# Eight gather buffers, earlier expert weights and rows loaded once in a graph network with experts

## The chip, the cores and the metric

The kernel runs on one core of one Trainium2 chip as a single launch. The metric is the device time of the whole execution, in microseconds. Each time is a median of runs on the same chip; the lowest and the highest stand beside it. The profile is one execution taken by the hardware profiler.

## The reference

A vector of 256 features for each of 3125 nodes passes eight residual parts: four graph layers and four expert layers. Two of the parts matter here. Both contain an attention over the neighbours of each node.

```python
# part L1_ffn: a graph attention chooses the experts (4 heads, 4 experts)
h = (x_flat @ W_gat).reshape(M, HEADS, NUM_EXPERTS)          # 16 numbers for a node
e = leaky_relu(a_src[src] + a_dst[dst], 0.2)                 # one score for edge and head
ee = exp(e - segment_max(e, dst)[dst])
alpha = ee / (segment_sum(ee, dst)[dst] + 1e-16)
agg = segment_sum(h[src] * alpha[:, :, None], dst) + b_gat   # self loops included
for ei in range(4):                                          # all experts for all nodes
    out += g[ei] * (gelu(x @ W1[ei] + b1[ei]) @ W2[ei] + b2[ei])

# part L3_gnn: graph attention, 8 heads of 32; then L3_ffn: 8 experts, top 2
alpha = segment_softmax(leaky_relu(a_src[src] + a_dst[dst], 0.2))
x = x + relu(segment_sum(h[src] * alpha[:, :, None], dst) + bias)
x = x + sum(combine[:, e] * (gelu(norm(x) @ w1[e] + b1[e]) @ w2[e] + b2[e]) for e in range(8))
```

The attention of L1_ffn has 65,536 edges and one loop for each node. That of L3_gnn has 100,000 edges.

## The kernel before

The nodes stand in 25 tiles of 128, one node on each partition. The program is a row of stages. A stage opens its own buffers and semaphores, writes one instruction list per engine, and closes with a barrier of all engines. What one stage does late, no other stage can hide. Within a stage the engines are tied together by counting semaphores alone; the helper `when` waits for a value that is worked out from loop registers.

An early stage sorts the edges by target on the chip and writes a table for each of the two attentions: blocks of `SLOTS` = 8 neighbours for each of the 128 nodes of a tile. `base_row` holds the first block of each tile, and at index NT the total. A tile of the router attention has two or three blocks, one of the head attention four to six. Unused slots of the table hold an index out of bounds, and the gather skips them. Since the loops round up, the table needs empty blocks behind the last one; a DMA from `empty` writes eight of them (one for each table, both waited for on `padded`).

**Stage l1p** (`prepare`) normalises x for the experts and leaves it transposed in `c.xt`. **Stage l1f** (`prepare`) makes the 16 features and the two scores of each node. It writes them to `rows`, sorted for gathering, and to `own_rows`, in the order of the tiles, with 24 numbers a row.

**Stage l1a** (`attend_beside_experts`) does the router's attention beside its experts:

- SP loads block indices for a ring of `BUFFERS` = 4 buffers, then the expert weights (`w1` and `w2`, 2 MB each, and four small bias loads and `b2`). After that it loops over blocks: it waits until a block's eight gathers have landed, signals `arrived`, and loads the indices of the block four later.
- POOL (GpSimd) loops over blocks, rounded up to the ring's length: it waits for `idx_in` and for `freed` (VectorE is done with the buffer), and issues eight indirect DMAs, each of 128 rows of 96 bytes (L2652).
- VectorE runs tiles. In `tile` it waits for the tile's own row and makes the softmax's start state by five operations (L2790 to L2796), which are the self loop. For each block, `edges` computes scores (from L2804), a running maximum and the differences `d`, signals `shifted`, waits for the exponentials on `weighed`, multiplies (L2819, after which the buffer is `freed`) and sums. Behind the first block of each tile but the first stands `empty`, which adds `b2` to the experts' output of the turn before.
- ScalarE runs the same tiles. `attend_tile` waits for `self_free`, issues the dynamic DMA of the own row into one of two slots of `self_rows` (L2709), and computes one exponential a block. Between them stand the experts' four Gelu steps of the turn and, in `store`, the store of y of the turn before. It ends with a wait for the own row. Exponential and Gelu take turns, so ScalarE reloads its function table.
- TensorE runs 20 turns (4 experts, 5 groups of 5 tiles), tied to `hidden` and `used`. So tiles 0 to 19 run beside a turn, and tiles 20 to 24 run without.
- At the end SP writes `found` to `by_gate` in 3200 pieces, and POOL gathers it back by `place` in 25 indirect DMAs.

**Stage l3a** (`attend_heads_beside_experts`) has the same skeleton with rows of 264 numbers. SP loads the four indices (L2218), then all weights of the last eight experts. VectorE fills the four buffers with `FLOOR` (L2397), waits for `loaded`, and handles the tiles. `valued` counts two products a block (L2428), and the second frees the buffer. The experts' work for a group of finished tiles runs beside the next group's attention; L2540 adds an expert's output to x. The last group is a single tile. POOL issues the stores of the finished tiles to `out_dram` (L2261), all behind the gathers in its own order, since they stand behind its loop.

Both loops of POOL and SP have `(total + BUFFERS) // BUFFERS` turns of `BUFFERS` blocks.

## Time and profile before

| | us |
|---|---|
| median of 3 runs | 5790.37 (5789.03 to 5790.59) |
| profiled execution, its own time | 5781.05 |
| span of the profiled execution | 5779.6 |
| TensorE, VectorE, ScalarE, GpSimd busy | 2908.9, 3171.6, 1642.9, 2183.8 |

The costliest groups of instructions on POOL and around the two stages, from the page (line, engine, operation, output<-input, count, then busy us and the mean of one in ns, then idle before and who ended most of it):

```profile
L2253 POOL DMA_INDIRECT l3a_got<-rows,l3a_idx x928 | 976.6, 1052 | 528.4 <-issue 286.9
...
L2652 POOL DMA_INDIRECT l1a_got<-rows,l1a_idx x512 | 510.4, 997 | 318.5 <-issue 159.5
...
L2686 PE MATMUL ps<-l1a_w,l1a_h 128*128 128x256 f32 x800 | 232.3, 432 | 224.1 <-issue 168.3
```

At the start of l3a, the first memset of a gather buffer and the issue of the four index loads on SP's queue (start, duration, engine, then in brackets the idle time before it and who ended it):

```profile
4158.77 1.82 DVE L2397 MEMSET l3a_got<- 128x2112 f32 x1 [0.41 <-issue]
4158.81 1.75 SPq L2218 DMA_DIRECT2D l3a_idx<-table_main  x4
```

Read the groups with the count in mind: 512 gathers are 64 blocks of eight, and the "issue" time of 159.5 us over 512 is the 0.3 us between two gathers. "issue" is time for which the profile shows no wait: the engine's own sequencer took it. A name with a q behind it (SPq, ACTq, DVEq) is an engine's sequencer, which waits, counts and issues DMAs; that time is not in the engine's busy time.

The stages of interest by time: l1p from 2085 to 2128.5, l1f to 2219.5, l1a to 3058 (the placing gathers behind it last until 3090), l3p from 4097 to 4158, l3a from 4158 to 5780.

### The profile page before, as it was taken

Reading aid. Unit: us, or ns where it says so; the run is one execution under the profiler, and the core shown is the slowest. Engines: PE = TensorE matmul, PEld = TensorE weight load, DVE = VectorE, ACT = ScalarE, POOL = GpSimd, SP = SyncE. Lnnn points to the kernel's source line nnn. Section 1 sums busy time; section 2 is a strip of 40 time slices with the busy share of each in tenths; the row PEclk is TensorE's granted clock in tenths of the full one; section 3 lists DMA queues with packets and bytes.
Section 4 is the critical chain, followed back from the end, with each engine's and each line's share of the span. In section 5 each row is a group of like instructions: output and inputs, shape, how many; then the busy total and the mean of one; then the engine's idle time right before and its main releaser. Section 6 shows DMA issues by size and latency. Waiting matters only on the chain. (4 is left out here: it accounts for less than half of the span.)

```text
span 5779.6 us, 67813 instructions
## 1 busy us (share of the span) xinstructions
PE 2908.9 (50%) x15435; PEld 2113.2 (37%) x15474; DVE 3171.6 (55%) x7705; ACT 1642.9 (28%) x2993; POOL 2183.8 (38%) x2146
## 2 busy tenths in 40 slices
PE   0430065895995952566730489958301132343446
PEld 0320064784884841344520234446200111122224
DVE  8876386674776561222224554442455656676663
ACT  0322042773771211223310254322101222222221
POOL 1036212001001526566562100015366656666662
PEclk9999999997996975777865799979655566666678
DMA  0311154543433211111113634432323322332210
GB/s 29 68 32 31 8 195 159 170 131 117 133 95 106 66 57 41 21 25 25 30 23 99 233 128 159 167 98 65 127 71 82 80 68 70 82 79 78 65 43 23
DMA packets 332190, 488.33 MB, mean 84 GB/s; under 512 B 159589, under 2 KB 250259, under 8 KB 330134
## 3 DMA queue, kind: packets, MB, share of 16 engines
q1 hardware_dynamic: 192198, 269.65, 14.9%
q0 software_dynamic: 92304, 177.29, 11.8%
q10 hardware_dynamic: 47552, 39.98, 2.1%
q14 instruction: 100, 0.82, 0.0%
q8 instruction: 36, 0.59, 0.0%
HBM read 375.91 MB, written 137.24 MB: 89 GB/s over the span
## 5 line engine op out<-in xcount | busy, mean ns | idle before, releaser
L2253 POOL DMA_INDIRECT l3a_got<-rows,l3a_idx x928 | 976.6, 1052 | 528.4 <-issue 286.9
L2348 PE MATMUL ps<-l3a_xt,l3a_w 128*128 128x512 f32 (+1 forms) x448 | 268.8, 761 | 739.8 <-ACT l3a_h L2292 492.0
L2652 POOL DMA_INDIRECT l1a_got<-rows,l1a_idx x512 | 510.4, 997 | 318.5 <-issue 159.5
L1581 PE MATMUL ps<-l0a_all_rows,l0a_w 128*128 128x257 f32 x2500 | 556.5, 382 | 28.2 <-DVE l0a_w L1699 28.2
L1581 PEld LDWEIGHTS ps<-l0a_all_rows,l0a_w 128*128 128x128 f32 x2500 | 475.8, 191 | 101.7 <-issue 31.9
L1972 PE MATMUL ps<-l2a_table,l2a_count 128*128 128x512 bf16 x1837 | 411.3, 384 | 61.1 <-DVEq L2067 59.1
L2348 PEld LDWEIGHTS ps<-l3a_xt,l3a_w 128*128 128x128 f32 x448 | 112.0, 276 | 875.6 <-issue 875.4
L2277 ACT ACT_TABLE_LOAD x99 | 127.0, 1283 | 904.5 <-DVEq L2419 583.4
L2686 PE MATMUL ps<-l1a_w,l1a_h 128*128 128x256 f32 x800 | 232.3, 432 | 224.1 <-issue 168.3
L1972 PEld LDWEIGHTS ps<-l2a_table,l2a_count 128*128 128x128 bf16 x1875 | 185.2, 99 | 287.5 <-issue 72.1
L1508 ACT ACTIVATE l0a_low<-ps,l0a_factors x650 | 254.1, 509 | 86.7 <-PE ps L1571 79.1
L2675 PE MATMUL ps<-xt,l1a_w 128*128 x640 | 220.0, 501 | 99.5 <-DMA l1a_b<-in_L_ffn_b_dram 54.8
L2686 PEld LDWEIGHTS ps<-l1a_w,l1a_h 128*128 128x128 f32 x800 | 168.4, 214 | 273.7 <-issue 251.5
L2358 PE MATMUL ps<-l3a_w,l3a_h 128*128 128x256 f32 x800 | 202.9, 410 | 124.1 <-DVEq L2543 93.0
L2428 DVE TENSOR_TENSOR l3a_v<-l3a_got,ps 128x1024 f32 x224 | 263.0, 1215 | 3.6 <-issue 2.9
L2358 PEld LDWEIGHTS ps<-l3a_w,l3a_h 128*128 128x128 f32 x800 | 163.2, 207 | 173.5 <-issue 151.1
L2675 PEld LDWEIGHTS ps<-xt,l1a_w 128*128 128x128 f32 x640 | 140.7, 223 | 187.1 <-issue 145.8
L1090 POOL DMA_INDIRECT rows<-own_rows,node x50 | 48.8, 975 | 416.1 <-DVEq L958 404.2
L2436 DVE TENSOR_TENSOR l3a_v<-l3a_v x112 | 141.1, 1259 | 116.1 <-issue 101.0
L1699 DVE TENSOR_TENSOR l0a_w<-l0a_w,l0a_held 128x1280 f32<-128x1280 f32 x130 | 192.9, 1485 | 13.4 <-DVE xt L1734 13.4
L1882 POOL DMA_DIRECT2D l2a_seen<-l2a_state x13 | 9.1, 704 | 468.3 <-DMA l2a_state<-l2a_seen 398.5
L2713 ACT ACT_TABLE_LOAD x53 | 68.0, 1283 | 351.6 <-issue 239.2
(965 smaller groups left out, 6576.1 us busy)
## 6 DMA issues: line engine op xcount, KB each, us to landing
l0a_held<-counts SPq DMA_DIRECT2D x130, 640.0 KB
counts<-count_held SPq DMA_DIRECT2D x13, 3200.0 KB, 9.7
l2a_held<-counts SPq DMA_DIRECT2D x65, 640.0 KB
l3a_got<-rows,l3a_idx POOLq DMA_INDIRECT x928
l_y<-l1a_y_sb ACTq DMA_DIRECT2D x20, 640.0 KB
l2a_table<-rows SPq DMA_DIRECT2D x16, 640.0 KB
l2a_state<-l2a_seen SPq DMA_DIRECT2D x1, 9984.0 KB
l2a_seen<-l2a_state POOLq DMA_DIRECT2D x12, 768.0 KB, 6.0
```

The source lines that it names most:

```text
L1508: ins = act.activation(low_at(n * Q + q, h), spread_of(n, W, 2 * W), ACT.Copy, scale=factors[:, C, at:at + 1])
L1581: ins = pe.matmul(sums_of(n, k, D + 1), w[:, at, k * P:(k + 1) * P], all_rows[:, at, 1:RW], start=(at == 0), stop=False)
L1699: dve.tensor_tensor(chunk(q), chunk(q), held_of(n, q), ALU.mult).then_inc(weighed, 1)
L1972: ins = pe.matmul(ps[:, bass.ds(parity(b, g) * G + k, 1), :].rearrange("p o n -> p (o n)"), count[:, at, k * P:(k + 1) * P], table[:, part ...
L2253: pool.indirect_dma_start(out=got[:, at:at + RW], out_offset=None, in_=rows[:, :], in_offset=bass.IndirectOffsetOnAxis(ap=idx[:, a, k:k + ...
L2348: ins = pe.matmul(ps[:, m, 0:size * P], w1[:, x, k, m * P:(m + 1) * P], xt[:, 0:size, k, :], start=(k == 0), stop=(k == KT - 1))
L2358: ins = pe.matmul(ps[:, 2 + j // 2, (j % 2) * D:(j % 2 + 1) * D], h[:, x % 2, m, j * P:(j + 1) * P], w2[:, x, m, :], start=(m == 0), stop= ...
L2428: dve.tensor_tensor(valued_of(b)[:, lo:hi, :, 0:DH], buffer(b)[:, lo:hi, 0:D].rearrange("p s (h d) -> p s h d", h=H), p[:, lo:hi, :].unsqu ...
L2436: ch(dve.tensor_tensor(rows[:, 0:4, :, :], rows[:, 0:4, :, :], rows[:, 4:8, :, :], ALU.add))
L2652: pool.indirect_dma_start(out=got[:, at:at + RW], out_offset=None, in_=rows[:, :], in_offset=bass.IndirectOffsetOnAxis(ap=idx[:, a, k:k + ...
L2675: ins = pe.matmul(ps[:, 2 * (m % 2) + q, 0:(hi - lo) * P], w1[:, x, k, m * P:(m + 1) * P], xt[:, bass.ds(i * C + lo, hi - lo), k, :], star ...
L2686: ins = pe.matmul(ps[:, 4 + j // 2, (j % 2) * D:(j % 2 + 1) * D], h[:, m, j * P:(j + 1) * P], w2[:, x, m, :], start=(m == 0 and j % 2 == 0 ...
```

## The change

1. **Rings of eight.** `BUFFERS` = 4 becomes `RING` = 8 in both attention stages: index slots, gather buffers, their semaphores, the first index loads, and in l3a the memsets. The loops of POOL and SP now round up to `(total + 7) // 8` turns of eight blocks. The tables get two empty pads each instead of one, and room for them (`blocks_of`).
2. **Weights ahead.** A new class `Ahead` holds the buffers of the router's expert weights. Their seven DMAs are issued on SP in stage l1p, behind its own loads, and stage l1a no longer has them. The buffers live across the three stages.
3. **Own rows once.** All 25 tiles' own rows come in one DMA into `self_all`, issued by SP in front of the index loads. VectorE makes `ref_all` (leaky relu of the self score) and `init_all` (ones, and the own features) for all tiles in four operations. A tile's prologue is now two copies. ScalarE loses the wait for `self_free`, the dynamic DMA and the wait for `self_in`; `self_free` and `self_in` no longer exist.
4. **One more wait.** `store` on ScalarE now waits on `y_out` until the store before last has landed.

```diff
-BUFFERS = 4
+RING = 8
+class Ahead:
+    def __init__(self, nc, stack, name, w_in, b_in, w_out, b_out):
...
+        self.landed, self.count = nc.alloc_semaphore(f"{name}_landed"), 3 + E
+    def load(self, sp):
+        w_in, b_in, w_out, b_out = self.sources
+        sp.dma_start(self.w1[:, :, :, :], w_in.rearrange("e (k p) n -> p e k n", p=P)).then_inc(self.landed, 16)
+        sp.dma_start(self.w2[:, :, :, :], w_out.rearrange("e (k p) n -> p e k n", p=P)).then_inc(self.landed, 16)
+        for x in range(self.E):
+            sp.dma_start(self.b1[:, x, :], b_in[x, :].rearrange("(k p) -> p k", p=P)).then_inc(self.landed, 16)
+        sp.dma_start(self.b2[:, :, :], b_out.rearrange("(o e) n -> o e n", o=1).broadcast_to([P, self.E, D])).then_inc(self.landed, 16)
...
# the tables
-                    sp.dma_start(s.table[bass.ds(total * (P * SLOTS), P * WIDE), 0].rearrange("(p s) -> p s", s=WIDE), empty[:, :]).then_inc(s.padded, 16)
+                    for k in range(2):
+                        sp.dma_start(s.table[bass.ds((total + k * SLOTS) * (P * SLOTS), P * WIDE), 0].rearrange("(p s) -> p s", s=WIDE),
+                                     empty[:, :]).then_inc(s.padded, 16)
-                    sp.wait_ge(s.padded, 16)
+                    sp.wait_ge(s.padded, 32)
...
# prepare, SP, behind its loads
+                    if ahead is not None:
+                        ahead.load(sp)
...
# both attention stages
-                with pool.Fori(0, (total + BUFFERS) // BUFFERS) as q:
-                    for a in range(BUFFERS):
+                with pool.Fori(0, (total + (RING - 1)) // RING) as q:
+                    for a in range(RING):
...
# l3a, POOL and VectorE
-                        when(pool, c, valued, q * (2 * BUFFERS) + (2 * a + 2))
+                        when(pool, c, valued, q * (2 * RING) + (2 * a + 2))
-                for a in range(BUFFERS):
+                for a in range(RING):
                     ch(dve.memset(buffer(a), FLOOR))
...
# l1a, SP
+                sp.dma_start(self_all[:, :, :], own_rows.rearrange("(t p) w -> p t w", p=P)).then_inc(loaded, 16)
-                    sp.dma_start(w1[:, :, :, :], w_in.rearrange("e (k p) n -> p e k n", p=P)).then_inc(weights_in, 16)
-                    sp.dma_start(w2[:, :, :, :], w_out.rearrange("e (k p) n -> p e k n", p=P)).then_inc(weights_in, 16)
-                    for x in range(E):
-                        sp.dma_start(b1_sb[:, x, :], b_in[x, :].rearrange("(k p) -> p k", p=P)).then_inc(weights_in, 16)
-                    sp.dma_start(b2[:, :, :], b_out.rearrange("(o e) n -> o e n", o=1).broadcast_to([P, E, D])).then_inc(b2_in, 16)
...
# l1a, ScalarE (the added wait is in store)
-                    when(act, c, self_free, t + 1)
-                    act.dma_start(self_rows[:, bass.ds((t % 2) * RW, RW)], own_rows[bass.ds(t * P, P), 0:RW]).then_inc(self_in, 16)
-                    when(act, c, self_in, (t + 1) * 16)
+                    when(act, c, y_out, turn * 16 + 32)
...
# l1a, VectorE, before the tiles
+                dve.wait_ge(weights_in, 16 * ahead.count)
+                ch.add(dve.tensor_tensor(ref_all[:, :, :], own_el, own_er, ALU.add))
+                ch.add(dve.memset(init_all[:, :, 0:H], 1.0))
+                ch.add(dve.tensor_copy(init_all[:, :, H:H + VW], own_h))
+                ch(dve.scalar_tensor_tensor(ref_all[:, :, :], ref_all[:, :, :], SLOPE, ref_all[:, :, :], ALU.mult, ALU.max))
...
# l1a, VectorE, each tile
-                    when(dve, c, self_in, (t + 1) * 16)
-                    ch.add(dve.tensor_copy(er_of[:, :], own(t, VW + H, RW)))
-                    ch(dve.tensor_tensor(top[:, :], own(t, VW, VW + H), own(t, VW + H, RW), ALU.add))
-                    ch.add(dve.scalar_tensor_tensor(e[:, SLOTS, :], top[:, :], SLOPE, top[:, :], ALU.mult, ALU.max))
-                    ch.add(dve.memset(den, 1.0))
-                    ch.add(dve.tensor_copy(acc, own(t, 0, VW)))
+                    ch.add(dve.tensor_copy(e[:, SLOTS:SLOTS + 1, :], ref_all[:, at_t, :]))
+                    ch.add(dve.tensor_copy(both[:, :].unsqueeze(1), init_all[:, at_t, :]))
                     ch.join()
-                    dve.sem_inc(self_free, 1)
...
-        return -(-edges // SLOTS) + 3 * NT + 4 * BUFFERS + 3 * SLOTS
+        return -(-edges // SLOTS) + 3 * NT + 2 * RING + 5 * SLOTS
...
-        prepare(nc, c, "l1p", c.x, None, D, ready=wmat, add=True)
+            ahead = Ahead(nc, held, "l1w", a["L1_ffn_W1"], a["L1_ffn_b1"], a["L1_ffn_W2"], a["L1_ffn_b2"])
+            prepare(nc, c, "l1p", c.x, None, D, ready=wmat, add=True, ahead=ahead)
```

## Rows read from the trace of the kernel before

**Rows 1.** Busy time by window: stage l1p, stage l1a, stage l3a's attention.

```profile
core 0: us, PE busy (x) PEld busy (x) DVE busy (x) ACT busy (x) POOL busy (x), PEclk, DMA share, GB/s
2085.00:2128.50 43.50, 31.93 (x150) 27.26 (x150) 31.70 (x111) 8.86 (x22) 0.00 (x0) 0.80 0.00 1
2219.50:3058.00 838.50, 446.58 (x1440) 309.06 (x1440) 205.84 (x1043) 209.08 (x318) 510.38 (x512) 0.73 0.16 28
4158.00:5660.00 1502.00, 421.83 (x1200) 254.52 (x1201) 943.11 (x2049) 310.27 (x498) 977.48 (x929) 0.62 0.28 74
```

**Rows 2.** Waits, l1a then l3a: who waits <- for whom: us, count, mean.

```profile
POOL l1a_got L2652 <- DVEq L2819: 158.6, 21, 13.7
...
DVE l1a_er_of L2791 <- DMA l1a_self_rows<-own: 142.0, 11, 19.6
...
DVE l1a_er_of L2791 <- issue: 90.1, 11, 14.0
...
POOL l3a_got L2253 <- DVE l3a_v L2428: 233.8, 30, 17.8
```

**Rows 3.** Timeline, POOL, first gather of two bursts: start, duration, [idle before <- releaser].

```profile
2480.37 0.99 POOL L2652 DMA_INDIRECT l1a_got<-rows,l1a_idx  x1 [6.37 <-DVEq L2819]
...
2517.70 0.99 POOL L2652 DMA_INDIRECT l1a_got<-rows,l1a_idx  x1 [6.42 <-DVEq L2819]
```

**Rows 4.** Timeline, PE, DVE and ACT between those bursts, 2500 to 2516.

```profile
2502.70 0.59 PE L2686 MATMUL ps<-l1a_w,l1a_h 128*128 128x256 f32 x1 [2.53 <-issue]
...
2504.06 0.17 DVE L2791 COPY l1a_er_of<-l1a_self_rows 128x4 f32 x1 [9.96 <-issue]
...
2504.80 0.70 ACTq L2709 DMA_DIRECT2D l1a_self_rows<-own  x1
...
2512.56 0.19 DVE L2804 TENSOR_TENSOR l1a_e<-l1a_got,l1a_er_of 128x32 f32<-128x32 f32 x1 [7.82 <-issue]
...
2514.65 5.54 PE L2675 MATMUL ps<-xt,l1a_w 128*128 x12 [0.62 <-issue]
2514.72 1.28 ACT L2713 ACT_TABLE_LOAD   x1 [20.25 <-issue]
```

**Rows 5.** Timeline, start of l1a.

```profile
2224.24 12.87 SPq L2627 DMA_DIRECT2D l1a_b<-in_L_ffn_b_dram  x4
...
2240.94 7.05 PE L2675 MATMUL ps<-xt,l1a_w 128*128 x16 [54.76 <-DMA l1a_b<-in_L_ffn_b_dram]
```

**Rows 6.** Timeline, start of l3a: VectorE's first operation of blocks 0, 3, 4 and 5.

```profile
4183.63 0.23 DVE L2413 TENSOR_TENSOR l3a_e<-l3a_got,er 128x64 f32<-128x64 f32 x1 [13.56 <-issue]
...
4227.40 0.23 DVE L2413 TENSOR_TENSOR l3a_e<-l3a_got,er 128x64 f32<-128x64 f32 x1 [8.58 <-issue]
...
4242.41 0.22 DVE L2413 TENSOR_TENSOR l3a_e<-l3a_got,er 128x64 f32<-128x64 f32 x1
...
4250.29 0.22 DVE L2413 TENSOR_TENSOR l3a_e<-l3a_got,er 128x64 f32<-128x64 f32 x1
```

**Rows 7.** Timeline, VectorE at the end of l1a, tiles 21 to 24.

```profile
2970.44 0.17 DVE L2791 COPY l1a_er_of<-l1a_self_rows 128x4 f32 x1 [1.16 <-DVE l1a_found L2837]
...
3017.29 0.17 DVE L2791 COPY l1a_er_of<-l1a_self_rows 128x4 f32 x1 [0.86 <-issue]
...
3028.05 0.18 DVE L2837 TENSOR_TENSOR l1a_found<-l1a_both,l1a_bias 128x16 f32 x1 [0.77 <-issue]
...
3046.11 0.19 DVE L2804 TENSOR_TENSOR l1a_e<-l1a_got,l1a_er_of 128x32 f32<-128x32 f32 x1 [10.88 <-remote]
...
3053.58 0.17 DVE L2837 TENSOR_TENSOR l1a_found<-l1a_both,l1a_bias 128x16 f32 x1 [0.16 <-DVE l1a_both L2836]
```

**Rows 8.** Timeline, VectorE at the end of l3a.

```profile
5529.36 2.35 DVE L2428 TENSOR_TENSOR l3a_v<-l3a_got,ps 128x1024 f32 x2
...
5621.91 1.66 DVE L2540 SCALAR_TENSOR_TENSOR x<-ps,l3a_g_now,x 128x256 f32 x4 [5.42 <-remote]
...
5684.74 1.66 DVE L2540 SCALAR_TENSOR_TENSOR x<-ps,l3a_g_now,x 128x256 f32<-128x256 f32 x4 [25.11 <-remote]

```

More of the change, by code:

```diff
@@ L2158, in attend_heads_beside_experts @@
         chain_sem, loaded, weights_in, arrived = (sem(n) for n in ("chain", "loaded", "weights_in", "arrived"))
[L2159 to L2160 removed]
+        idx_in = [sem(f"idx_in_{a}") for a in range(RING)]
+        gathered = [sem(f"got_{a}") for a in range(RING)]
         shifted, exped, weighed, valued = (sem(n) for n in ("shifted", "exped", "weighed", "valued"))
@@ L2395, in _ @@
                 dve.memset(warmed[:, :], 0.0).then_inc(warm, 1)
-                for a in range(BUFFERS):
+                for a in range(RING):
                     ch(dve.memset(buffer(a), FLOOR))
@@ L2559, in _, with attend_beside_experts @@
                 ch.restart()
-def attend_beside_experts(nc, c, name, table, base_row, rows, own_rows, bias, tiny, place, agg, w_in, b_in, w_out, b_out, y):
+def attend_beside_experts(nc, c, name, table, base_row, rows, own_rows, bias, tiny, place, agg, ahead, y):
     H, DH = 4, 4
@@ L2619, in load @@
                         "(p s) -> p s", s=SLOTS)).then_inc(idx_in[a], 16)
[L2621 removed]
+                for a in range(RING):
                     load(a, a)
[L2623 to L2630 removed]
+                with sp.Fori(0, (total + (RING - 1)) // RING) as q:
+                    for a in range(RING):
                         when(sp, c, gathered[a], (q + 1) * (16 * SLOTS))
                         sp.sem_inc(arrived, 1)
[L2634 to L2637 removed]
+                        load(q * RING + (RING + a), a)
+                for a in range(RING):
+                    when(sp, c, idx_in[a], ((total + (RING - 1)) // RING + 1) * 16)
                 sp.wait_ge(closed, 1)
@@ L2642, in _ @@
             def _(pool):
-                total = pool.value_load(base_row[0:1, c.NT:c.NT + 1], min_val=1, max_val=blocks - 2 * BUFFERS)
+                total = pool.value_load(base_row[0:1, c.NT:c.NT + 1], min_val=1, max_val=blocks - 2 * RING)
                 last_node = pool.to_reg(c.N - 1)
-                with pool.Fori(0, (total + BUFFERS) // BUFFERS) as q:
-                    for a in range(BUFFERS):
+                with pool.Fori(0, (total + (RING - 1)) // RING) as q:
+                    for a in range(RING):
                         when(pool, c, idx_in[a], (q + 1) * 16)
-                        when(pool, c, freed, q * BUFFERS + (a + 1))
+                        when(pool, c, freed, q * RING + (a + 1))
                         for k in range(SLOTS):
```

92 lines of the change are left out of this document (44 added, 48 removed).

## The prediction

> **What bounds the kernel now.** I read the stage windows first, then who waits for whom in the two attention stages, then single tile changes in the timeline. The kernel is a row of stages with a barrier between them, so a gain counts only in its own stage. The change works in two: l1a (the router attention, 838.5 us) and l3a (head attention, some 1500 us and a tail). In both no engine is busy two thirds of the time: GpSimd (POOL) 510 of 838 us and 977 of 1502 us, TensorE and VectorE less [rows 1]. POOL issues the gathers, 510.38 us for 512 in l1a, 1.0 us each [rows 1], and 0.3 us of issue between them, so 8 of them, one block, take 10.4 us.
>
> A deeper ring pays where the consumer waits for a gather. It does not. In l1a POOL is the one that waits, 158.6 us in 21 waits, for VectorE to free a buffer; VectorE's own waits are for its own rows (142.0 us, 11 times, and 90.1 us of issue) [rows 2]. In l3a POOL waits 233.8 us for a buffer [rows 2]. The ring is full, not empty.
>
> What costs time is odd. POOL starts a burst at 2480.37 and gathers three blocks without a pause, some 31 us; the next starts at 2517.70, after 6.42 us of waiting [rows 3]. So a tile of three blocks takes 37.3 us, burst and pause. Late in a burst all other engines crawl: VectorE idles 9.96 us before its row copy at 2504.06 and 7.82 us more before its first edge operation at 2512.56, and ScalarE's table load comes after 20.25 us of "issue"; meanwhile TensorE stands before single matmuls of 0.59 us, 2.53 us before the one at 2502.70. At 2514.65, some 3.4 us after the burst's end (2517.70 less 6.42), TensorE runs 12 matmuls in 5.54 us [rows 4]. I call this the crawl; the traces show it after 10 to 25 us of unbroken gathers and not its cause.
>
> **The change, part by part.**
> *Weights earlier.* TensorE begins at 2240.94, held by the bias loads, whose issue alone takes 12.87 us on SP [rows 5]; VectorE waits for the same loads, until some 2242. Now SP enters its loop at once, and block 0, whose gathers start as SP issues the biases (2224.24) and last 10.4 us, can be used about 2236.5, some 5.6 us sooner. But the next blocks follow at 10.4 us, so block 1 is not ready before some 2247, about when VectorE comes to it now. Gain 1 us (bounds 0 and 6). The move puts 4 MB and some 14 us of issue on SP's queue in l1p, where SP has nothing else and the DMA share is 0.00 over 43.5 us [rows 1]; its last load needs to land only by 2236, some 110 us later. Cost 0; the 12.87 us of bias issue and what goes with it if that cover were gone. The one load of all own rows replaces 25 small ones; it is first on SP's queue, 12 us or more before block 0 is there: 0. The longer memset (0.7 us more) hides there too.
>
> *Tile change in l1a.* Gone per tile: ScalarE's wait, dynamic DMA and second wait, VectorE's wait and three of its five operations. These operations take 0.2 us or less each (the row copy 0.17 [rows 4]); what they cost is turns in the crawl (ScalarE's DMA holds its queue 0.70 us [rows 4], which I take for each instruction of ScalarE and VectorE) and the row's DMA, queued behind the y store. Since the period is burst plus pause, only the pause can shrink. Of 6.4 us, 3.4 us are the crawl's end, which stays; then ScalarE's table load, its exponential and VectorE's three operations until the buffer is free, the other 3.0 us [rows 3, 4]. With the row's DMA gone ScalarE has 5 of about 11 turns less before that exponential, so it often falls before the crawl ends. I take 2.5 us for each of the 20 tiles beside experts: -50. Bounds: 0 (TensorE's 20 starved instructions come last instead) and 158.6 (no pause at all). The new wait for the store before last stands in front of ScalarE's store and, behind it, the next tile's exponentials; that store was issued a tile (27 us or more) earlier, so 0.
>
> *Rings of eight.* In the steady state buffer b+8 is asked for when b is freed, as b+4 was: 0. What differs is the start and the end. At the start POOL runs four more blocks, 41.7 us, without a pause, and the others crawl longer. In l3a's first burst VectorE starts block 0 at 4183.63, block 3 at 4227.40 and block 4 at 4242.41, and block 5, after it, at 4250.29 [rows 6]: 14.6 us a block in the crawl against 7.9. In 41.7 us that is 2.9 blocks for 5.3, a loss of 19 to 20 us in each stage (bounds 0 and 42): +20 and +20.
> At the end of l1a the last eight blocks, tiles 21 to 24, took 83.1 us from 2970.44 to 3053.58, with gathers nearly to the end: tile 24's first edge operation stood 10.88 us, to 3046.11, until they were over. Uncrawled, a tile takes some 10.7 us (3017.29 to 3028.05, one tile's first operation to its last) [rows 7], four 43. With eight buffers the last three blocks are still gathered once tile 20 frees its buffers, 31 us past it, so I leave 10 us of crawl: -31 (bounds -41 and -10).
>
> *l3a besides.* Four more index loads (the four of now hold SP's queue 1.75 us, in the table's fence) stand before the weights' issue, after which SP first signals a block (VectorE's first block is at 4183.63): +2. Four more memsets (1.82 us each, the same fence) stand in front of that same wait, in which VectorE idles 13.56 us [rows 6]: 0 (bound +8). VectorE handles 112 blocks, POOL gathers 928 / 8 = 116; rounded up to eights it is 112, so 32 gathers vanish. Gathers run into the last tile's own time, and the stores of `out_dram` follow them without a pause. Behind them VectorE stands 25.11 us until 5684.74 [rows 8]; about 4 us of it is TensorE's work. Now the last gathers are block 111's, which start when block 103's product (5529.36 [rows 8]) is done, so POOL is free by 5545 and stores 13 or 17 tiles then: -21 at the tail, -10 for VectorE's gaps in the last tile, 5.42 us at 5621.91 [rows 8] and one like it, +8 for the same stores crawling earlier (bounds 0 and 21).
> The second pad of each table: +1.
>
> Sum: l1a -1 -50 +20 -31 = -62; l3a +2 +20 -21 -10 +8 = -1; pads +1; -62 us. The profiled execution took 5781.05 us, span 5779.6, 9.3 us under the median; it comes to 5719, the median to **5728 us**.
>
> The Trainium skill speaks against the crawl: "SBUF — State Buffer", section "Who interferes with whom", says DMA never contends with a compute engine, and that only GpSimd's descriptor generation is starved, by VectorE. The trace disagrees: gathers stay at 0.99 us while the others slow down [rows 3, 4]. By the page the two first bursts would cost nothing, and the sum would be 40 us lower, 5688; as far as the trace bears it out, 5 of the forecast's 59 in 100.
>
> **Rivals.** *Pauses vanish* (18%): the removed row load was the whole pause. For it: 142.0 and 90.1 us of waits [rows 2]; against: crawl and starved TensorE. l1a is then POOL's 64 blocks of 10.4 us from 2224, 666 us, and 40 us for what the ring still holds: it ends at 2930, not 3054. 124 us less, 5666.
> *Slower: bursts merge* (13%): once ScalarE's exponential comes before a burst's end, POOL starts the next three blocks at once, and the crawl lasts through them. It decides when the others progress at under half speed in 62 us bursts: then a merged pair of tiles takes as long as two now. Transitions 0, first bursts +42 each, end -31, l3a tail -21 -10 +8, start +2, pads +1, -1: +32, 5822.
> *No change* (10%): the tile change is off the path, since TensorE's starved matmuls end last, and the rings' two ends cancel: -62 + 50 = -12, less if the tail's stall only moves (+13): 5791.
> Forecast 59%, own range 5685 to 5770.
>
> **Numbers.** 0.2% is 11.6 us, about what a measurement can tell from no change. The range reaches down near the vanished pauses and up over no change, with 8 and 9 of 100 left outside: 5655 to 5805. Faster: 0.59 x 0.97 and all of the vanished pauses, 0.75. Slower: the merged bursts and a little of no change, 0.14. Same 0.11.
>
> **What would show it.** Right: POOL's pauses in l1a of 3 to 5 us instead of 6.4, and no wait of VectorE for own rows; tiles 21 to 24 in about 52 us; block starts in l3a's first 150 us later than before by 20 us; 896 gathers in l3a, and the step from the last `l3a_stats` to the next sum under 10 us. Wrong: pauses unchanged (the path is TensorE), bursts of six blocks with a period over 75 us (merging), or first bursts no slower (the crawl does not grow with the burst).

## The result, and the profile after

| | before, us | after, us |
|---|---|---|
| median | 5790.34 (5789.03 to 5790.59, 4 runs) | 5906.74 (5899.09 to 5912.77, 4 runs) |
| span of the profiled execution | 5779.6 | 5910.9 |

Ratio 1.0204, 95% interval 1.0188 to 1.0220: 116 us slower, where 62 us faster was forecast and the range ended at 5805.

The two traces laid over each other, stage by stage, give the 131.3 us between the spans: 2.3 us up to l1a's start, 66.9 in l1a, 2.8 between its end and l3a's start, and 59.3 from there. Times since each stage's first memset, from VectorE's operations in the timelines:

| us since the stage's start | before | after |
|---|---|---|
| l1a: first burst of gathers | 9 blocks, 93.5 us | 14 blocks, 145.8 us |
| l1a: tile 1 ends | 120.3 | 174.3 |
| l1a: tile 20 ends | 749.1 | 852.7 |
| l1a: tile 24 ends | 833.6 | 900.5 |
| l3a: first burst of gathers | 7 blocks, 74.1 us | 14 blocks, 149.2 us |
| l3a: tile 1 starts | 114.9 | 171.5 |
| l3a: last block starts | 1477.9 | 1559.1 |
| l3a: end of the kernel | 1621.3 | 1680.6 |

So l1a lost 54 us in the first burst and 50 in its steady state and got 37 back at the end. l3a lost 57 in the first burst and 25 on the way and got 22 back. (The first tiles are larger than was said: tile 0 has five blocks in l1a and seven in l3a.)

Busy time by window in the changed kernel, l1a and l3a's attention (core 0: us, then busy time and count of each engine, TensorE's granted clock, DMA share, GB/s), to lay beside [rows 1]:

```profile
2221.50:3123.00 901.50, 437.47 (x1440) 307.23 (x1440) 199.50 (x972) 207.74 (x318) 512.20 (x512) 0.70 0.12 21
4230.00:5795.00 1565.00, 427.05 (x1158) 257.45 (x1159) 934.80 (x2024) 308.92 (x495) 954.60 (x913) 0.61 0.27 72
```

Nobody works more: POOL's 512 gathers are busy for 512.2 us as before, VectorE's work in l1a is 6 us less, the clock a little lower. What grew is idle time, and the waits say whose (who waits <- for whom: us, times, longest), beside [rows 2]:

```profile
DVE l1a_y_sb L2800 <- DMA l0e_got<-done: 360.7, 20, 34.6
...
POOL l1a_got L2670 <- DVEq L2834: 201.5, 20, 15.8
...
POOL l3a_got L2278 <- DVE l3a_v L2453: 259.7, 31, 20.4
```

VectorE's wait for own rows is gone, as the change says. In its place stands one before `empty` (L2800), 360.7 us in 20 waits. The name behind the arrow is a wrong guess of the profile: by the code these are the waits for `used`, the signal of TensorE's last output matmul of the turn, and for an earlier store of y. In the case below all stores of y issued so far had landed by 2564.2. Timeline of the changed kernel, TensorE, ScalarE and VectorE from 2557 to 2597 (start, us, engine, line, idle before <- releaser):

```profile
2557.53 8.80 PE L2704 MATMUL ps<-l1w_w,l1a_h 128*128 128x256 f32 x40
...
2585.98 0.58 PE L2693 MATMUL ps<-xt,l1w_w 128*128 x1 [2.22 <-issue]
...
2589.81 1.28 ACT L2744 ACT_TABLE_LOAD   x1 [19.51 <-DMA l0e_got<-done]
2590.12 1.62 DVE L2800 TENSOR_TENSOR l1a_y_sb<-ps,l1w_b 128x512 f32 x3 [16.76 <-DMA l0e_got<-done]
...
2592.47 0.19 DVE L2819 TENSOR_TENSOR l1a_e<-l1a_got,l1a_self_all 128x32 f32 x1 [0.73 <-DVE l1a_y_sb L2800]
...
2593.61 1.28 ACT L2728 ACT_TABLE_LOAD   x1 [0.72 <-DVEq L2824]
...
2595.36 0.29 DVE L2828 TENSOR_TENSOR l1a_v<-l1a_got,l1a_p 128x128 f32<-128x128 f32 x1 [1.59 <-ACT l1a_p L2728]
```

And POOL's two burst starts around it:

```profile
2555.34 1.00 POOL L2670 DMA_INDIRECT l1a_got<-rows,l1a_idx  x1 [10.26 <-DVEq L2834]
...
2596.59 0.99 POOL L2670 DMA_INDIRECT l1a_got<-rows,l1a_idx  x1 [10.27 <-DVEq L2834]
```

The last output matmul starts at 2565.95, and VectorE passes its wait for it at 2589.65, just before ScalarE passes one for a product whose matmul started at 2568.1. Until then VectorE has no operation for 16.76 us and ScalarE none for 19.51, until 3.5 us after the burst's last gather (2596.59 less 10.27 is 2586.3).

Are the two engines frozen, or do they wait for a signal? The trace also holds the times at which semaphores were updated. The update of `used` that VectorE waited for is recorded at 2589.62, 23.7 us after the start of its matmul, and the two of `product` at 2589.72 and 2589.81. So by the record they wait for TensorE's signals, and these come late. In all of l1a 36 of the 40 updates of `used` are recorded. Half of them come 12 us or more after the start of the matmul before them, and 29 more than 5 us after it. In the kernel before it is 22 of 40 that come more than 5 us after it. Whether the signal is late, or the matmul itself, whose end is modelled, the trace does not tell. Nor is this all of the crawl: VectorE's gap before 2512.56 in [rows 4] ends without any update from TensorE (the next is recorded at 2514.87).

The period of the tiles is 41.25 us against 37.3 in [rows 3]; the burst is still 31 us, and the pause went from 6.4 to 10.3 us. Of those 10.3, the crawl's end is 3.5 as before. Behind it stand now three adds of `empty` (1.62 us), and then a whole block: scores, table load, exponential, product. Before, the same place held only the second half of a block whose scores were already done (2512.56 in [rows 4]); `empty` came behind POOL's restart, under the burst. The other engines do not work less between two bursts. They are at another point of the tile when the crawl catches them.

The first burst of l3a, VectorE's first operation of blocks 0, 3, 4, 5, 6 and 7 and POOL's first burst, beside [rows 6]:

```profile
4259.74 0.23 DVE L2438 TENSOR_TENSOR l3a_e<-l3a_got,er 128x64 f32<-128x64 f32 x1 [7.96 <-issue]
...
4304.27 0.23 DVE L2438 TENSOR_TENSOR l3a_e<-l3a_got,er 128x64 f32<-128x64 f32 x1 [7.91 <-issue]
4329.67 0.23 DVE L2438 TENSOR_TENSOR l3a_e<-l3a_got,er 128x64 f32<-128x64 f32 x1 [9.30 <-issue]
4354.25 0.23 DVE L2438 TENSOR_TENSOR l3a_e<-l3a_got,er 128x64 f32<-128x64 f32 x1 [7.88 <-issue]
4380.24 0.23 DVE L2438 TENSOR_TENSOR l3a_e<-l3a_got,er 128x64 f32<-128x64 f32 x1 [8.58 <-issue]
4402.57 0.23 DVE L2438 TENSOR_TENSOR l3a_e<-l3a_got,er 128x64 f32<-128x64 f32 x1 [0.50 <-DVE l3a_acc L2469]
```

```profile
4233.44 1.04 POOL L2278 DMA_INDIRECT l3a_got<-rows,l3a_idx  x1 [7.65 <-DVEq L2423]
...
4395.50 1.73 POOL L2278 DMA_INDIRECT l3a_got<-rows,l3a_idx  x1 [12.87 <-DVE l3a_v L2453]
```

POOL gathers from 4233 to 4382.6 without a pause. Deep in the burst VectorE takes 25 us a block, not 14.6, while POOL takes 10.6. One such block was in the trace of before too. From block 2 to block 3 it took 24.5 us (4202.91 to 4227.40), where blocks 0 to 2 together had taken 19.3:

```profile
4202.91 0.23 DVE L2413 TENSOR_TENSOR l3a_e<-l3a_got,er 128x64 f32<-128x64 f32 x1 [6.21 <-issue]
```

Each block that VectorE frees gives POOL another one, so eight buffers became a burst of 14 blocks.

At the end of l3a the step that was expected behind [rows 8] is there. The last tile's sums, with 1.94 us before the one that waited 25.11:

```profile
5806.83 1.66 DVE L2565 SCALAR_TENSOR_TENSOR x<-ps,l3a_g_now,x 128x256 f32<-128x256 f32 x4 [0.41 <-DVE x L2485]
...
5812.69 1.66 DVE L2565 SCALAR_TENSOR_TENSOR x<-ps,l3a_g_now,x 128x256 f32<-128x256 f32 x4 [1.94 <-PE ps L2383]
```

### The profile page after: what moved, and what is told of

It reads as the page before. It is cut to its first block and busy times, and to the rows that moved or that the text cites. A ratio compares the mean times of both kernels' runs of the same rounds, so it can differ in the third digit from the quotient of the medians.

```text
span 5910.9 us, 67346 instructions
## 1 busy us (share of the span) xinstructions
PE 2914.1 (49%) x15435; PEld 2119.0 (36%) x15474; DVE 3170.5 (54%) x7638; ACT 1642.8 (28%) x2993; POOL 2145.7 (36%) x2114
## 5 line engine op out<-in xcount | busy, mean ns | idle before, releaser
L2278 POOL DMA_INDIRECT l3a_got<-rows,l3a_idx x896 | 937.9, 1047 | 540.1 <-issue 272.7
L2670 POOL DMA_INDIRECT l1a_got<-rows,l1a_idx x512 | 512.2, 1000 | 367.0 <-DVEq L2834 201.5
L2693 PE MATMUL ps<-xt,l1w_w 128*128 x640 | 264.6, 553 | 392.2 <-ACT l1a_h L2744 205.0
L2693 PEld LDWEIGHTS ps<-xt,l1w_w 128*128 128x128 f32 x640 | 153.3, 244 | 499.8 <-issue 467.7
L2383 PE MATMUL ps<-l3a_w,l3a_h 128*128 128x256 f32 x800 | 211.3, 422 | 112.5 <-issue 48.1
L2800 DVE TENSOR_TENSOR l1a_y_sb<-ps,l1w_b 128x512 f32 (+1 forms) x60 | 32.4, 596 | 360.7 <-DMA l0e_got<-done 360.7
L2704 PE MATMUL ps<-l1w_w,l1a_h 128*128 128x256 f32 x800 | 179.3, 383 | 36.0 <-issue 35.6
L2704 PEld LDWEIGHTS ps<-l1w_w,l1a_h 128*128 128x128 f32 x800 | 153.9, 193 | 58.3 <-issue 36.9
```

Of the source, the lines that this page charges most:

```text
L2278: pool.indirect_dma_start(out=got[:, at:at + RW], out_offset=None, in_=rows[:, :], in_offset=bass.IndirectOffsetOnAxis(ap=idx[:, a, k:k + ...
L2383: ins = pe.matmul(ps[:, 2 + j // 2, (j % 2) * D:(j % 2 + 1) * D], h[:, x % 2, m, j * P:(j + 1) * P], w2[:, x, m, :], start=(m == 0), stop= ...
L2670: pool.indirect_dma_start(out=got[:, at:at + RW], out_offset=None, in_=rows[:, :], in_offset=bass.IndirectOffsetOnAxis(ap=idx[:, a, k:k + ...
L2693: ins = pe.matmul(ps[:, 2 * (m % 2) + q, 0:(hi - lo) * P], w1[:, x, k, m * P:(m + 1) * P], xt[:, bass.ds(i * C + lo, hi - lo), k, :], star ...
L2704: ins = pe.matmul(ps[:, 4 + j // 2, (j % 2) * D:(j % 2 + 1) * D], h[:, m, j * P:(j + 1) * P], w2[:, x, m, :], start=(m == 0 and j % 2 == 0 ...
```

## The experiments

The chips differ. Each set of runs was compared with the kernel before on its own chip. I call the chip of the result A. The others were B to G, six different ones; A may be one of them.

| chip | kernel before, median | l1a, last tile ends | tile of three blocks |
|---|---|---|---|
| A (result) | 5790 | 834 | 37.4 |
| B | 5752, and 5776 in a later set | 830 (count alone) | 37.5 (count alone) |
| C | 5328 | 665 | 31.2 |
| D | 5325 | 666 | 31.2 |
| E | 5325 | 666 | 31.2 |
| F | 5789 | 830 | 37.5 |
| G | 5790 | not traced | not traced |

In l1a of chip B I use the kernel with the count alone (below); its loops have the same turns in that stage as before's.

On A, B, F and G the other engines crawl beside gathers; on C, D and E they do not, and the same program takes 425 to 465 us less. This is the largest finding. Only B was used at two times, and it crawled at both, so that a chip keeps to its kind is likely and not shown. TensorE's signals tell the two kinds apart. In the changed kernel on chip D every recorded update of `used` and `product` in l1a comes 0.39 to 0.65 us after the start of its matmul. There is no late one on C and E either.

Each kernel has one trace, and on the crawling chips runs of one kernel differ by more than on the others: the kernel before took 5774 to 5824 us on F and 5318 to 5330 on D. So a trace there shows one execution, and medians have to bear it out.

**Ring alone (chip B).**

```diff
-BUFFERS = 4
+BUFFERS = 8
-(total + BUFFERS) // BUFFERS
+(total + (BUFFERS - 1)) // BUFFERS
```

and the pads. 

> The kernel before with rings of eight alone (and the pads and loop counts that go with them). Ring theory: the first burst of gathers grows from 9 to 14 blocks in l1a and from 7 to 14 in l3a whatever else is changed, so tile 1 of l1a ends some 54 us late and tile 0 of l3a some 56 us late; l3a ends 58 us late in all, l1a loses 54 and gets 36 back at its end; periods of l1a's tiles stay at 37.4 us: about 5790 + 58 + 18 + 4 = 5870. Rival (the ring alone also sets the phase in which a tile's burst begins): l1a's periods go to 41.3 us as in the changed kernel, 5906 or more. Second rival (the own rows' part makes the long first burst of l1a): l1a as before, 5790 + 58 + 4 = 5852 or less.

Measured: 5823.05 against 5752.37, ratio 1.0140 (1.0080 to 1.0201). Tile 1 of l1a ends at 174.2, tile 1 of l3a starts at 172.6. The ring alone makes the bursts of 14 blocks (in l3a 13, and after 1.9 us one more). The tiles' period is 40.9 us, though block 0 starts at 25.4 as in before (24.7); so the ring by itself also moves the phase, which is the point of a tile at which the crawl sets in. l1a's last tile ends at 872.2. The ring theory had the time (71 us slower, 80 expected) and was wrong on the period.

```profile
2466.15 0.99 POOL L2654 DMA_INDIRECT l1a_got<-rows,l1a_idx  x1 [9.97 <-DVEq L2821]
...
2507.07 0.99 POOL L2654 DMA_INDIRECT l1a_got<-rows,l1a_idx  x1 [10.00 <-DVEq L2821]
```

(POOL's burst starts in l1a of that kernel.)

**The rest with rings of four (chip B).** The changed kernel with

```diff
-RING = 8
+RING = 4
```

> The changed kernel with rings of four: weights ahead, own rows once, start states at once, the added wait. Phase theory: without the row load VectorE reaches the next tile's first block before the others freeze, and what is left behind the freeze is the experts' output sum and a whole block; periods of l1a's three-block tiles are 41.3 us against 37.4 with four buffers too: 5790 + 49 = 5839. Ring theory: the longer periods come from the ring; with four buffers they stay at 37.4 or get shorter as forecast: 5730 to 5790. l3a as before in both, within 5 us.

Measured: ratio 1.0023 (0.9994 to 1.0053). l3a: tile 1 starts at 114.8 as before. l1a: 40.9 us a tile, last tile at 876.2. So this half moves the phase too, by itself. The expectation for l3a was missed: it ends at 1560.8, 60 us earlier than on A, which hides the loss of l1a in the ratio. The count explains some 24 us of it (below), the rest is open.

**Rings of two.** The changed kernel with

```diff
-RING = 8
+RING = 2
```

First on chip B: 

> The changed kernel with rings of two. Ring theory, if the loss grows with the blocks gathered before VectorE's first: the first bursts get shorter than before's (9 and 7 blocks), some 20 us less in each stage against a ring of four; against it, a gather can start only when the block before the last is done, so VectorE now waits for gathers of 10.4 us each after a pause: up to 5 us a block in l1a if nothing else changes. 40 us faster to 150 us slower than the ring of four; faster would say that four was too deep as well.

Measured: ratio 0.9942 (0.9912 to 0.9972). Tile 1 of l1a ends at 105.1, the last at 844.1. That is 46 us under the same kernel with rings of four, so shallower was better still on this chip. Its periods are mixed, 34.8 us for two tiles and then mostly 41. Chip E, without crawl, with a control: 

> Control with a trace, on whatever chip this call gets. Where the other engines slow down beside gathers: tile 1 of l1a ends 120 us after the stage's start and three-block tiles take 37.4 us, as in the first trace; if they take 41 us here, the 37.4 was one of two ways to fall in step, and the 4 us a tile that the changed kernel took more were not the change's. Where they do not slow down: 31.2 us a tile.

> The changed kernel with rings of two. Where nothing slows down, GpSimd is the bound in l1a and a ring of two must still keep it busy: VectorE takes some 4 to 6 us for a block of 10.4 us, so buffers come free in time, l1a ends within 10 us of before's 666 us; in l3a a block takes VectorE 7.9 us, and tiles' ends and the experts' adds hold it for 10 to 20 us at once, which two buffers do not cover: 20 to 100 us more, ratio 1.00 to 1.02. Where engines slow down: ratio 0.99 to 0.997, as on the first chip that had it.

Measured: 5478.38 against 5325.20, ratio 1.0292 (1.0274 to 1.0309). l1a lost 8 us, l3a 138: VectorE now waits for SP's signal that a block has landed (who waits <- for whom: us, times, longest).

```profile
DVE l3a_e L2438 <- SPq L2261: 212.8, 67, 18.6
```

The expectation for l3a, 20 to 100, was too low. Two buffers are no cure: they gain on one chip and lose on the other.

**A break after each block (chip B).** In the changed kernel, after the eight gathers in both stages:

```diff
+                        when(pool, c, gathered[a], (q + 1) * (16 * SLOTS))
```

> The changed kernel with rings of eight, but GpSimd waits after each block's eight gathers until they have landed, before it issues the next block. If the slowing of the other engines comes from gathers in a row without any break, a break of 1 to 2 us every 10.4 us ends it: the first bursts cost nothing, l1a's tiles follow GpSimd at some 36 us (3 x 12) and 24 us, 900 us become about 780, and l3a gains some 80: 5700 or less. If the slowing comes from how much of the time gathers fill, the break changes little: each block costs 1 to 2 us more where GpSimd is the bound, 5906 + 60 to 200.

Measured: 5749.04, ratio to before 1.0010 (0.9981 to 1.0040), some 150 us under the changed kernel. The first bursts' loss is gone with rings of eight: tile 1 of l1a ends at 110.8 and tile 1 of l3a starts at 112.5. l1a goes at POOL's pace, 12.8 us a block, and ends at 807.4, about as early as with the same break on a chip without crawl (814.1 with rings of four, below). None of TensorE's recorded updates in l1a comes more than 2.9 us after its matmul's start. l3a ends at 1614.5, no better than before: there the breaks cost what they save. So the expectation of 5700 or less was missed. The kernel before with the count alone is about as fast on this chip (5749.62, below). POOL at two breaks in l1a:

```profile
2571.79 0.99 POOL L2671 DMA_INDIRECT l1a_got<-rows,l1a_idx  x1 [3.16 <-issue]
...
2584.04 0.99 POOL L2671 DMA_INDIRECT l1a_got<-rows,l1a_idx  x1 [2.14 <-issue]
```

A break of 2.1 to 3.4 us every 10.4 us, in which the gathers also land, ends the crawl's cost in l1a, with eight buffers. This is the run that ties the loss to unbroken gathers rather than to the ring.

**Four kernels on chip C, where nothing crawls.** A control: 

> The kernel before, unchanged, as a control with a trace on the same chip as the three beside it. If the period of l1a's three-block tiles (37.4 us in its first trace) belongs to the kernel, it is 37.4 us here too; if it belongs to the way the engines happen to fall in step, it may be 41 us as in the rings of two, four and eight of the changed kernel, and then no part of the change made it.

It gave 31.2 us a tile of three blocks and 5324 us. The question that it was asked could not be answered there. The break (the same added line) in l1a alone, with `RING = 4`: 

> The changed kernel with rings of four, and GpSimd waits in l1a alone for the landing of each block before it issues the next. Burst theory: l1a follows GpSimd at 12.6 us a block, some 807 us to the last tile against 876 without the waits; l3a stays as with rings of four without waits, 1561 us. Sum against the ring of four: -69, 5684. Rival (pacing moves l3a or the chip's other parts as well, or ring four paces worse than eight): over 5720.

Measured: 5468.05 against 5328.38, ratio 1.0266 (1.0252 to 1.0280). l1a's last tile ends at 814.1 against 665.4: without a crawl the break is pure cost. The weights' part alone, that is the kernel before with

```diff
-        prepare(nc, c, "l1p", c.x, None, D, ready=wmat, add=True)
+            prepare(nc, c, "l1p", c.x, None, D, ready=wmat, add=True, ahead=ahead)
...
-                pe.wait_ge(weights_in, 16 * (2 + E))
+                pe.wait_ge(weights_in, 16 * ahead.count)
-                dve.wait_ge(b2_in, 16)
+                dve.wait_ge(weights_in, 16 * ahead.count)
```

and l1a's own loads of them taken out: 

> The kernel before with the weights of l1a loaded in l1p and nothing else of the change (rings of four, own rows tile by tile). If the fetch ahead costs or gives nothing beyond l1a's start: block 0 of l1a starts some 7 us earlier, the last tile ends within 6 us of before's 833.6 us after the stage's start, and the time is within 10 us of before. If the tiles' periods go to 41 us here too, the start's phase alone sets them: +43 us in l1a.

Measured: ratio 0.9997 (0.9988 to 1.0006), block 0 starts 8.5 us earlier, the last tile ends at 666.6. A fill in place of the wait:

```diff
+                        pool.memset(filler[:, :], 0.0).then_inc(gapped, 1)
+                        when(pool, c, gapped, q * RING + (a + 1))
```

> The changed kernel with rings of four, and in l1a after each block of gathers GpSimd fills a spare tile of 128x2048 (some 1.7 us) and waits for that, and not for the landing. If the others are slowed because gathers follow one another without a break, a break of 2 us without any landing helps as much as the wait does: last tile of l1a at some 800 to 815 us, 5690. If it is the gathers that are still under way that count, the fill does little: 860 us or more, 5740 to 5780.

Measured: ratio 1.0314 (1.0299 to 1.0330), last tile at 839.3. On a chip without crawl this says nothing of its cause, and no run shows it on the other kind.

**The changed kernel again (chip D).** 

> The kernel before once more, as the control beside the changed kernel on one chip. On the chip of the last call none of the other engines slowed down beside gathers and l1a went at GpSimd's pace (31.2 us a tile of three blocks, 20.8 of two), 5324 us; where they do slow down, 37.4 us a tile and some 5750 to 5790 us.

> The changed kernel. If its whole loss comes from the other engines slowing down beside unbroken gathers: on a chip where they do not, the first bursts of 14 blocks cost nothing, l1a ends within 5 us of before's and l3a gives the 20 to 25 us of its shorter tail, ratio 0.995 to 0.999; on a chip where they do, ratio 1.01 to 1.02, tile 1 of l1a ends some 174 us and tile 1 of l3a starts some 172 us after its stage's start. If the loss has another cause in the rings themselves (gathers that wait for one another, a longer queue), it is slower by 1 to 2% on any chip.

Measured: 5325.14 against 5325.17, ratio 0.9999 (0.9989 to 1.0008). l1a's last tile ends at 666.7 against 666.0; its first burst is its only one, 512 gathers in 665.8 us. Busy time in l1a by window (columns as above) in the kernel before:

```profile
2156.00:2822.00 666.00, 383.72 (x1440) 290.99 (x1440) 206.71 (x1040) 207.05 (x318) 506.63 (x508) 0.80 0.19 35
```

and in the changed kernel:

```profile
2161.00:2828.00 667.00, 386.66 (x1440) 292.67 (x1440) 200.66 (x972) 207.07 (x318) 506.43 (x509) 0.80 0.16 28
```

POOL's waits for a buffer in l1a (who <- for whom: us, times, longest), before and then after:

```profile
POOL l1a_got L2652 <- DVEq L2819: 3.1, 10, 0.3
```

```profile
POOL l1a_got L2670 <- DVEq L2834: 5.8, 19, 0.3
```

POOL's waits for buffers, 158.6 us in [rows 2], are 3.1 here with the same code. VectorE waits for gathers, as one would expect of a stage that POOL bounds. So without the crawl the change costs nothing, and its whole loss hangs on the crawl.

**Count and rows (chip F, with crawl).** 

> Control with a trace on this call's chip. Where the other engines slow down beside gathers: three-block tiles of l1a take 37.4 us if that period is the kernel's own, 41 us if it is one of two ways to fall in step.

The control gave 37.5 us, 830.2 at the last tile: the period of 37 us is before's own on a second chip. The count alone is the second pair of lines of the first diff above, with rings of four and one pad: 

> The kernel before with the loops' turns rounded up without a spare turn: (total + 3) // 4 in place of (total + 4) // 4, so l3a issues 896 gathers in place of 928, and nothing else. The step of the prediction: the last 32 gathers and the stores behind them stood in the last tile's way, and from l3a's last block to the kernel's end it takes 120 us instead of 143. Where engines slow down beside gathers: 20 to 25 us faster, ratio 0.996. Where they do not: the end hides the stores anyway, ratio 1.000.

Measured: 5756.61 against 5789.37, ratio 0.9941 (0.9921 to 0.9960). From the last block to the end it takes 119.3 us against the control's 143.1. The sum that was late, in the control and then with the count:

```profile
5687.73 1.66 DVE L2540 SCALAR_TENSOR_TENSOR x<-ps,l3a_g_now,x 128x256 f32<-128x256 f32 x4 [25.12 <-remote]
```

```profile
5667.60 1.66 DVE L2540 SCALAR_TENSOR_TENSOR x<-ps,l3a_g_now,x 128x256 f32<-128x256 f32 x4 [1.94 <-PE ps L2358]
```

The rows' part, with the weights' load put back into l1a:

```diff
+                    ahead.load(sp)
-            prepare(nc, c, "l1p", c.x, None, D, ready=wmat, add=True, ahead=ahead)
+            prepare(nc, c, "l1p", c.x, None, D, ready=wmat, add=True)
```

> Own rows once with the start states at once and the added wait of the store, rings of four, the weights issued in l1a as before. Phase theory: where engines slow down, three-block tiles take 41 us and two-block tiles 30 us, as with rings of two and four of the changed kernel, and l1a ends 40 us later than the control's. If the weights' earlier start made that phase: 37.4 us and no loss. Where nothing slows down: GpSimd is the bound and l1a ends within 3 us of the control.

Measured: 5803.16 against 5789.37, ratio 1.0021 (0.9997 to 1.0044). In the traced execution the periods are some 37.2 us on average (the control's 37.8) and the last tile ends at 827.7 against 830.2: in it, rows once does not move the phase, and it hardly shortens the pause, which was the forecast's largest term. POOL's burst starts, control first:

```profile
2474.09 0.99 POOL L2652 DMA_INDIRECT l1a_got<-rows,l1a_idx  x1 [6.66 <-DVEq L2819]
...
2512.58 1.00 POOL L2652 DMA_INDIRECT l1a_got<-rows,l1a_idx  x1 [7.53 <-DVEq L2819]
```

```profile
2478.33 1.00 POOL L2672 DMA_INDIRECT l1a_got<-rows,l1a_idx  x1 [7.07 <-DVEq L2836]
...
2514.87 0.99 POOL L2672 DMA_INDIRECT l1a_got<-rows,l1a_idx  x1 [5.64 <-DVEq L2836]
```

But this execution (5765.93) was the shortest of ten, whose median is 5803. The kernel holds the count's gain too, and the kernel with the count alone took 5756.61 beside it. So by the medians the rows' part costs some 47 us on this chip, about what a move to the 41 us period costs in l1a (45 us in the next run). Where the other executions lose it is not traced, and whether the expectation was wrong stays open. VectorE's waits for own rows (172.2 us in the control) are gone in the trace, and POOL waits for buffers as long as before (155.0 us for 151.0): the idle time went elsewhere.

**The weights' part alone, with crawl (chip G).** 

> The kernel before with the weights of l1a loaded in l1p and nothing else, asked of a chip on which the other engines slow down beside gathers. If the earlier start of VectorE and TensorE in l1a is what puts the tiles into the 41 us period: tile 1 ends at 131 us instead of 120 to 124 after the stage's start, three-block tiles take 41 us, l1a ends some 45 us later than before, and the kernel is 40 to 50 us slower, ratio 1.007 to 1.009. If it needs the rows' part as well: 37.4 us a tile and ratio 1.000.

Measured: 5816.09 against 5789.92, ratio 1.0043 (1.0024 to 1.0061). Tile 1 ends at 131.5, tiles take 41.3 us, the last ends at 875.3.

```profile
2466.43 1.00 POOL L2667 DMA_INDIRECT l1a_got<-rows,l1a_idx  x1 [10.33 <-DVEq L2834]
...
2507.82 0.99 POOL L2667 DMA_INDIRECT l1a_got<-rows,l1a_idx  x1 [10.36 <-DVEq L2834]
```

With block 0 of the stage 8.5 us earlier, each of ten tiles takes 4 us more. The whole time grew by 26 us and not by the 45 of l1a; l3a's part varies from run to run, as said below.

**Count and whole change once more (chip B).** 

> The kernel before with turns rounded up without a spare one, on another chip. Where engines slow down beside gathers: 0.994 to 0.997 again, and 120 us from l3a's last block to the end instead of 143. Where they do not: within 0.1% of before, since the last gathers and stores then cost the last tile nothing (120 us from the last block to the end with 928 gathers too).

Measured: 5749.62 against 5776.06, ratio 0.9955 (0.9924 to 0.9986); 116.0 us from the last block to the end.

> The changed kernel beside it. Where engines slow down: ratio 1.015 to 1.022, the first burst of l1a and of l3a 14 blocks long and tiles of l1a at 41 us. Where they do not: 0.999 to 1.001. A ratio in between would mean that the slowing has degrees.

Measured: 5899.93, ratio 1.0208 (1.0152 to 1.0264). Tile 1 of l1a ends at 173.8, tile 1 of l3a starts at 173.6. The first bursts of chip A come back within some 2 us, and the ratio with them.

Chip B has a ratio for each step of the change, each against before in its own set: 0.9955 with the count, 1.0023 with weights and rows as well, 1.0208 with all. So the count gives 0.45%, weights and rows together cost some 0.7%, and the ring of eight costs some 1.85%, or 107 us. The ring alone with the count (1.0140) gives the same 1.85% the other way round. Each ratio is known to 0.3 to 0.6%.

Where engines crawl the count alone was faster than before on both chips (0.6% and 0.45%), and 150 us faster than the changed kernel beside it. It was not run on a chip without crawl. There the changed kernel, which has the same count, takes 120 us from the last block to the end, and so does before, so nothing is to be expected either way.

## Why the prediction was wrong, point by point

- *What bounds the kernel.* Right for the crawling chips: ring full, crawl late in a burst. The text said that the cause was not shown, and then priced everything as if its course were known.
- *Weights earlier: -1.* The failed step is "Gain 1 us (bounds 0 and 6)". The start itself went as worked out (block 0 earlier, block 1 about where it was). That an 8 us shift of the first block puts all later tiles at another point of the crawl was not among the bounds: +42 to +45 in l1a when done alone (875.3 against 833.6 on chip A, 830.2 on F).
- *Tile change: -50.* The failed step is the count of 2.5 us saved in each pause. Alone the rows' part gave 2 us in the stage in one short execution, and cost some 47 us by the medians; the pause of the changed kernel is 10.3 us, not 3.9. ScalarE and VectorE do not crawl at 0.7 us an instruction until the burst's end: [rows 4] already had gaps of 9.96 and 20.25 us. In the trace of after the longest such gaps end with late signals of TensorE, which fewer instructions of ScalarE do not bring sooner. In the pause stands what comes after the gap, and this is set by the phase. The rival "pauses vanish" was wrong on the same ground: the waits for own rows went, and POOL's pauses did not.
- *First bursts: +20 each.* The mechanism was right and the term mis-sized: 54 and 57. Two things were left out: the burst does not grow by four blocks but by five and seven, since blocks freed within it prolong it; and deep in it a block takes 25 us. The 14.6 us were a mean of three steps, 5.1, 14.2 and 24.5, that grow. The bound of 42 was no bound, since it took only four more blocks of burst.
- *Rings of eight, steady state: 0.* Failed in l1a. The ring alone gives the 41 us tiles too, as do the weights alone; so the 50 us that l1a lost there cannot be shared out among the parts, which do not add up (42 to 45 us alone, 50 together).
- *End of l1a: -31.* Right, 84.5 became 47.8, -37 us.
- *l3a's start, memsets, index loads, pads: +3.* Some 4 us for block 0 of l3a (29.5 against 25.3), and 5 before and between the stages: small, as said.
- *l3a's steady state: 0.* 25 us were lost between tile 1 and the last block on chip A. On chip B the kernel with the ring alone lost some 6 us there against the one with rings of four (its last block 63.7 us later, tile 1 57.8). This term is not settled: the same code varies by tens of microseconds in l3a on crawling chips (last block at 1477.9 on A, 1489.1 on F).
- *End of l3a: -21 -10 +8.* Right as a sum: 143.4 became 121.5 us from the last block to the end, and the count alone gave 24 us on F (143.1 to 119.3) and, on B, 116.0 us where A and F have 143. Its cause is the spare turn of gathers, not the deeper ring.
- *Rivals.* "Bursts merge" had the right sign and its price for the first bursts (42 each) was nearest, but its mechanism, a merging of later bursts, is not seen: the bursts of the three-block tiles stayed at 24 gathers. Its 5822 was 85 us short. The range left out the cases in which the first burst feeds itself and a pause grows.

The Trainium skill says in "SBUF — State Buffer", section "Who interferes with whom", that ScalarE and TensorE never wait on anyone. It speaks of the ports of that memory. On chips C, D and E the traces agree: TensorE's busy time in l1a is 383.7 us (chip D) and nothing slows beside 666 us of unbroken gathers. On A the other engines do slow down beside them ([rows 4]). Whether a port has part in that no trace shows, so the rule is not refuted there. Yet the prediction's sum by it, 5688, fails on the crawling chips. Nor did a gain of 1.8% come true on a chip without crawl: there the change is worth nothing (chip D, 0.9999), since POOL bounds l1a.

What stays open: what makes TensorE's signals late and the engines of some chips crawl beside gathers, and if it belongs to the chip. No trace shows a resource that is full then; the gathers take 1.0 us on both kinds. Loading of instructions does not look like it: the DMA queues that the profile calls instruction move 11 packets in l1a of the kernel before on A and 11 on D, and none between 2564.4 and 2590 in the gap shown above. Whether a break of idle time would do without the landing (the fill) was asked on a chip without crawl, and is open. So is what picks the period of 37.4 or 41 us.

## What to carry to other kernels

A full ring is no reason for a deeper one: where the producer disturbs the others while it runs, each buffer more prolongs its longest burst, and the consumer's own progress then feeds the burst. Before costing a saving inside a stall, look in the trace for the signal that ends it; if that comes from elsewhere, only the work behind it counts, and a shift of a few microseconds at a loop's start can change that for all later turns. Run a control with a trace on each chip. And set the time of the traced execution beside the median before you trust what the trace says of a part: one of them here was the shortest of ten.

## What the runs showed of the hardware that I had not expected

- The same program, with the same gathers of 1.0 us, takes 5325 us on three chips and 5752 to 5790 where the other engines slow down beside bursts of indirect DMAs from GpSimd.
- In such bursts TensorE still starts a matmul every 2.8 us, and the semaphore updates of its matmuls are recorded up to some 24 us after their start (29 of 36 of `used` over 5 us after it in l1a of the changed kernel). On chip D they are recorded after 0.39 to 0.65 us. In a burst of three blocks in l1a ScalarE and VectorE go on 3.5 us after its last gather.
- With a wait for the landing after each 8 gathers, a break of 2.1 to 3.4 us, no such update is later than 2.9 us, and the changed kernel is as fast as before (1.0010 against 1.0208 without breaks).
- The tiles of l1a run mostly with periods of about 37.4 or 41 us there. An earlier first block alone put them at 41, and so did a ring of eight alone with the first block where it was.
